# A recurrence over blocks of tokens: block transfers by column halves, and the border of a block run like its inside

## The reference, cut to what matters

```
Wx = einsum('bti,hi->bth', x, W)              # x: normalised tokens
Wx = batchnorm(Wx) * gamma + beta
def step(yt, wx_t):
    yt = sigmoid(wx_t + yt @ V.T)
    return (yt, yt)
_, ys = lax.scan(step, zeros, swapaxes(Wx, 0, 1))
out = x1 + ys                                 # x1: the residual stream, 16 images of 128 x 16384
```

## Time and profile before

| | |
|---|---|
| time, median of 3 runs (lowest, highest) | 5048.64 us (5047.34, 5053.07) |
| the profiled execution: time | 5051.68 us |
| its span | 5049.9 us |
| PE busy, granted clock over the span | 96%, 0.989 |
| DVE, ACT, POOL busy | 80%, 77%, 75% |
| the recurrence's 1024 steps | about 3879 to 5006 us of the span, then the last store |

### The profile page before, as it was taken

How to read it: one execution, slowest core, us unless ns; L and a number is a source line. 1 busy time by engine, 2 the same in 40 slices (tenths; PEclk the granted TensorE clock), 3 DMA queues, 4 the chain that set the end, 5 groups by cost and what they waited for, 6 DMA issues and landing times. The chain is left out here.

```text
span 5049.9 us, 147380 instructions
## 1 busy us (share of the span) xinstructions
PE 4850.0 (96%) x38766; PEld 4491.2 (89%) x38766; DVE 4028.0 (80%) x13465; ACT 3900.6 (77%) x10328; POOL 3787.5 (75%) x5133
## 2 busy tenths in 40 slices
PE   7999999999999999999999999999986999999996
PEld 6799999999999999999999999899876999999996
DVE  7899999999999999999999999999964444444442
ACT  5788888888888888888888888888874666666664
POOL 6688887888887878888887888888762666666764
PEclk9999999999999999999999999999998999999998
DMA  2355555555555545555554555555475689888897
GB/s 59 94 147 149 143 146 143 145 145 146 144 147 143 148 142 146 146 142 149 143 148 141 147 144 147 143 146 149 134 199 223 167 243 262 211 240 243 248 244 158
DMA packets 1692439, 821.25 MB, mean 163 GB/s; under 512 B 1095328, under 2 KB 1623584, under 8 KB 1689936
## 3 DMA queue, kind: packets, MB, share of 16 engines
q1 hardware_dynamic: 1690528, 816.80, 57.5%
q10 hardware_dynamic: 1584, 0.79, 0.1%
HBM read 413.17 MB, written 270.01 MB: 135 GB/s over the span
## 5 line engine op out<-in xcount | busy, mean ns | idle before, releaser
L502 POOL TENSOR_TENSOR x_t<-x_t,y 128x512 f32<-128x512 f32 x512 | 769.3, 1527 | 425.4 <-ACT y L436 425.4
L436 ACT ACTIVATE y<-bank,zbias 128x128 f32<-128x128 f32 x2112 | 776.9, 368 | 387.7 <-PE bank L402 255.5
L458 DVE TENSOR_TENSOR th_t<-x_t,bank 128x512 f32<-128x512 f32 x528 | 528.6, 1042 | 645.0 <-PE bank L373 563.8
L402 PE MATMUL bank<-y,VT 128*128 128x128 f32 x4216 | 869.2, 289 | 11.0 <-issue 10.3
L380 PE MATMUL bank<-th_t,WzT 128*128 128x128 f32 x4224 | 805.2, 277 | 13.0 <-DVE th_t L458 12.8
L662 PEld LDWEIGHTS bank<-WqT,xh 128*128 128x128 f32 x4096 | 538.7, 192 | 245.3 <-issue 245.3
L402 PEld LDWEIGHTS bank<-y,VT 128*128 128x128 f32 x4216 | 671.6, 189 | 59.7 <-issue 13.2
L787 ACT ACTIVATE thT<-bank,srstd 128x128 f32<-128x128 f32 x1920 | 548.6, 369 | 191.2 <-POOL srstd L878 190.9
L805 ACT ACTIVATE onT<-bank,orstd 128x128 f32<-128x128 f32 x1920 | 548.9, 369 | 135.9 <-POOL orstd L897 135.3
L380 PEld LDWEIGHTS bank<-th_t,WzT 128*128 128x128 f32 x4224 | 635.5, 193 | 20.3 <-DVE th_t L458 20.2
L919 POOL TENSOR_TENSOR rstd<-veps,minus_half 128x4 f32<-128x4 f32 x512 | 531.4, 1038 | 76.2 <-POOL veps L915 1.2
(11 more groups left out here) (150 smaller groups left out, 11285.5 us busy)
## 6 DMA issues: line engine op xcount, KB each, us to landing
xin<-in_x SPq DMA_DIRECT2D x512, 256.0 KB, 2.9
qin<-q_image SPq DMA_DIRECT2D x512, 256.0 KB, 2.7
x2in<-in_x SPq DMA_DIRECT2D x512, 256.0 KB, 2.9
x_scratch<-x1o SPq DMA_DIRECT2D x1024, 128.0 KB, 2.1
out<-x_t SPq DMA_DIRECT2D x256, 512.0 KB, 6.6
r_t<-r_scratch SPq DMA_DIRECT2D x51, 32.0 KB, 2.1
r_scratch<-rS SPq DMA_DIRECT2D x3, 256.0 KB, 20.9
r_scratch<-rS ACTq DMA_DIRECT2D x3, 256.0 KB, 21.5
```

Of the source, the lines that this page charges most:

```text
L402: pe.matmul(z_b[c][g % 2][:, u * CC:(u + 1) * CC], VT[:], last, start=False, stop=(u == GS - 1), skip_group_check=True).then_inc(pre_ps[c], 1)
L436: act.activation(y[c][:, g % RING, u, :], z_b[c][g % 2][:, u * CC:(u + 1) * CC], ACT.Sigmoid, bias=zbias[:]).then_inc(y_sb[c], 1)
L458: dve.tensor_tensor(th_t[c][:, g % 2].rearrange("p u (x q) -> p u x q", x=XP), x1_t[q][:, c * CC:(c + 1) * CC, h * GS:(h + 1) * GS].rearra ...
L502: pool.tensor_tensor(dst, dst, y[c][:, g % RING, :, :].rearrange("p u (x q) -> p q x u", x=XP), ALU.add).then_inc(slot_free[c], 1)
```

## The change

The load of a block is split into two DMAs, one for each column half, with semaphores of their own, and the stores count on a semaphore for each half. SP starts the stores of half 0 (sequences 0 to 7) when half 0's last add is done, and those of half 1 after half 1's; each half's load waits for its own half's stores. DVE waits for `x1_in` of each half at that half's first `scale`.

The border of a block is issued like its inside: `z_piece` of the next block's first group stands between the V matmuls of the last group, and the r pieces of the second group after its second step. DVE's order of work is the same as before, written without the special cases. The broadcast of r (`r_piece`) is one matmul for a group and half, as it was.

```
-            sp.dma_start(x1_t[p][:], x1_s[bass.ds(blk, 1)].rearrange("o c s t -> (o c) s t")).then_inc(x1_in[p], 16)
+            cols = slice(c * CC, (c + 1) * CC)
+            sp.dma_start(x1_t[p][:, cols, :], x1_s[bass.ds(blk, 1), :, cols].rearrange("o c s t -> (o c) s t")).then_inc(x1_in[p][c], 16)
...
-                    if stored is not None:
-                        sp.wait_ge(out_st[p], stored)
-                        settle(sp)
-                    load_x1(sp, blk, p)
+                    for c in range(2):
+                        if stored is not None:
+                            sp.wait_ge(out_st[p][c], stored)
+                            settle(sp)
+                        load_x1(sp, blk, p, c)
...
                     for c in range(2):
                         sp.wait_ge(slot_free[c], w * SWEEP + blk * NG + NG + RING)
                         settle(sp)
-                    src = x1_t[p][:].rearrange("c (b j) t -> c b j t", j=J)
-                    for b in range(B):
-                        sp.dma_start(out_v[bass.ds(blk, 1), :, b].rearrange("o c j t -> (o c) j t"), src[:, b]).then_inc(out_st[p], 16)
+                        for b in range(c * B // 2, (c + 1) * B // 2):
+                            sp.dma_start(out_v[bass.ds(blk, 1), :, b].rearrange("o c j t -> (o c) j t"), src[:, b]).then_inc(out_st[p][c], 16)
...
-                            if g + 1 < n:
+                            if g + 1 < n or ahead:
                                 z_piece(g + 1, u, c)
-                            if u == 1 and (g + 2 < n or ahead and g + 2 == n):
+                            if u == 1 and (g + 2 < n or ahead):
                                 r_piece(g + 2, c)
-                if ahead:
-                    for u in range(GS):
-                        for c in range(2):
-                            z_piece(n, u, c)
-                    for c in range(2):
-                        r_piece(n + 1, c)
...
-                    if g in (0, n) and c == 0:
-                        dve.wait_ge(x1_in[q], 16 * (loaded if q == p else loaded + 1 - p))
+                    if g in (0, n):
+                        dve.wait_ge(x1_in[q][c], 16 * (loaded if q == p else loaded + 1 - p))
```

More of the change, by code:

```diff
@@ L127, in build @@
         r_in = [sem(f"r_in{p}") for p in range(2)]
-        x1_in = [sem(f"x1_in{p}") for p in range(2)]
-        out_st = [sem(f"out_st{p}") for p in range(2)]
+        x1_in = [[sem(f"x1_in{p}{c}") for c in range(2)] for p in range(2)]
+        out_st = [[sem(f"out_st{p}{c}") for c in range(2)] for p in range(2)]
         start_ok = [sem(f"start_ok{c}") for c in range(2)]
@@ L308, in build, with load_x1 @@
         y0 = [yb[:].rearrange("p (x b j) -> p x b j", x=XP, j=J // XP) for yb in y_start]
-        def load_x1(sp, blk, p):
-            sp.dma_start(x1_t[p][:], x1_s[bass.ds(blk, 1)].rearrange("o c s t -> (o c) s t")).then_inc(x1_in[p], 16)
+        def load_x1(sp, blk, p, c):
+            cols = slice(c * CC, (c + 1) * CC)
+            sp.dma_start(x1_t[p][:, cols, :], x1_s[bass.ds(blk, 1), :, cols].rearrange("o c s t -> (o c) s t")).then_inc(x1_in[p][c], 16)
         def scan_dma(sp):
@@ L334, in loads @@
                     load_r(blk, p)
-                    if stored is not None:
-                        sp.wait_ge(out_st[p], stored)
-                        settle(sp)
-                    load_x1(sp, blk, p)
+                    for c in range(2):
[3 more added lines that the diff above has]
+                        load_x1(sp, blk, p, c)
                 def store(blk, p):
+                    src = x1_t[p][:].rearrange("c (b j) t -> c b j t", j=J)
                     for c in range(2):
@@ L353, in scan_dma @@
                         store(2 * k + p, p)
-                        loads(2 * k + 2 + p, p, w * SWEEP + WARM + (2 * k + p + 1) * NG, (stores + k + 1) * 16 * B)
+                        loads(2 * k + 2 + p, p, w * SWEEP + WARM + (2 * k + p + 1) * NG, (stores + k + 1) * 8 * B)
                 for p in range(2):
@@ L357, in scan_dma @@
                 for p in range(2):
-                    sp.wait_ge(out_st[p], (stores + NB // 2) * 16 * B)
-                    settle(sp)
+                    for c in range(2):
+                        sp.wait_ge(out_st[p][c], (stores + NB // 2) * 8 * B)
+                        settle(sp)
         def scan_tensor(pe):
@@ L466, in block_steps @@
                 for g in range(n):
-                    if g + 2 < n or ahead and g == n - 1:
+                    if g + 2 < n or ahead:
                         for c in range(2):
[L469 to L472, removed]
+                            scale(g + 2, c)
             for c in range(2):
@@ L580, in _ @@
             sp.wait_ge(gram_ps, B * NC)
-            load_x1(sp, NB - 1, 1)
+            for c in range(2):
+                load_x1(sp, NB - 1, 1, c)
             store_r(sp, 0)
```

## The result

The changed kernel takes 5064.9 us (median of 8 runs), the kernel before 5048.4 us in 8 runs beside it: the ratio is 1.0031, with a 95% interval from 1.0020 to 1.0042. It is slower by 0.31%, some 16 us. One disturbed run of 9189.5 us is left out of the comparison.

What follows compares the result with a forecast made beforehand. PE's order and the transfers were taken to bind at once. Blocks 1 to 14 +12.0, block 0 +0.4, block 15 -2.8, last stores -1.5: together +8.1 us on the median 5048.6, so 5057 us; range 5036 to 5068.

Steps and rivals of the forecast that it cites:

- border like inside, block there: Block border issued like its inside, nothing else late: 67.1 us a block, giving PE back 3.5 us a block.
- first store's issue: SP's first store at A + 1.73, A being the start of POOL's first add in a block's last group.
- gain of the transfers by halves: First load need not wait for the last store's landing: 0.7 us sooner, bounds 0 and about 1.4 us.
- half 1's scale starts: DVE starts half 1's scale at A + 66.0 (A: start of POOL's first add in a block's last group).
- 8 landing blocks, clock up: Eight blocks with no branch back ahead stop 3.4 us for half 1 in the last group: 70.5 us each.
- stop at a branch: PE's stop at its loop's end, at six borders, grows from 1.7 to 2.7 us; growth between 0 and 1.8.
- 6 branch blocks, clock up: Six blocks behind a branch back reach half 1 after it is ready, no second stop: 67.1 + 2.7 us each.
- slow stretches: PE's clock falls to 1.2 GHz at nearly every new stop, 1.3 us each; bounds 0 and 1.5.
- The clock that stays up: Rival: PE's clock does not fall at the new stops, all blocks take 70.5 us: 5043 us; chance 0.15.
- the transfers overlap better: Rival: half 1's landing moves 2.4 us, not 0.7, and the stop shrinks to 1.7 us: 5029 us; chance 0.13.
- The half loads at half speed: Rival: half-row loads run slowly, the load's 23 us become 43, each block grows by 20: +280 us; chance 0.02.
- The case of no gain in the transfers: Rival: transfers gain nothing, branch stop of 3.9 us, a full-price clock fall each time: 5072 us; chance 0.10.

Runs made afterwards that it cites:

- half of the stores: The changed kernel with 8 of each block's 16 stores left out, so half the output is never written and loads go out earlier: 5006.5 us, ratio 0.9914.
- the order alone: The kernel before, with whole-block transfers, given only the changed PE program (new order of the border): 5106.9 us, ratio 1.0113.
- the halves alone: The changed kernel, with transfers by halves, given PE's program of before (old order of the border): 5045.7 us, ratio 0.9990.
- half 1 late: The changed kernel with half 1's z matmuls and r piece in a block's last group put behind the last V matmul: 5029.0 us, ratio 0.9961.

## Why the prediction was right, and where its sizes were off

The mechanism is as it was put: what the border gave back, the block's landing and the branch took, and the slow clock behind the new stops added to it. The point, 5057 us, was 8 us short: +8 was forecast, +16 came. The result lies just above the band from 5048 to 5064 us to which the forecast gave 0.60, and almost midway between the point and the 5072 us of a rival; the prediction held a change within 0.2% (0.46) a little likelier than a slower kernel (0.40). So the sign and the path are right, and the size isn't. For the profiled execution the steps compare like this:

| step | forecast | measured |
|---|---|---|
| border like inside, block there (half of the stores) | 67.1 us a block | 67.2 |
| first store's issue | A + 1.73 | A + 1.76 |
| gain of the transfers by halves | 0.7 us | 0.6 |
| half 1's scale starts | A + 66.0 | A + 66.15 |
| from that start to the next A, clock up | 1.05 + 3.4 = 4.45 | 4.53 (three blocks) |
| 8 landing blocks, clock up | 70.5 | 70.65 (66.12 + 4.53) |
| stop at a branch | 2.7 | 3.2 |
| 6 branch blocks, clock up | 67.1 + 2.7 = 69.8 | 70.7 |
| slow stretches | 14, 1.3 us each: 18.2 | 9, 16.2 us together |
| blocks 1 to 14 | +12.0 | +16.4 |
| up to block 0's A | +0.4 | +2.3 |
| block 15 | -2.8 | -3.6 |
| last store | -1.5 | -1.5 |

**The term that failed in size is the branch back.** The stop was to grow from 1.7 to 2.7 us, taken between 0 and 1.8 more; it grew to 3.2, near the upper end. That is 0.5 us in each of six blocks, +3.1. And that PE comes to half 1 there after it is ready, and does not stop again, was not quite so: where no slow stretch follows the branch (blocks 9 and 11), the last group takes 4.65 us (4584.20 to 4588.85) and not 4.2, because PE is still early. It waits 0.27 us for half 1 there, and the group is some 0.5 us longer in all, +1.0 for the two. In the other four the last group takes 4.2 us. Some 0.2 us more a block are left, mostly in the group behind the stop, which takes 4.45 us beside it (block 9: 7.48 - 3.03). Together +5.2.

The runs that show it: the order alone has the same 19.4 us at branches, the halves alone 9.7. The trace shows why, in its records of the transfers that load instructions (q8). At each branch one of them brings 16 KB. Behind block 4 it begins at 4231.74, 0.65 us after PE stopped; in the kernel before it began at 4229.69, 0.60 us ahead of the stop at 4230.29. It is the lone entry early in each of these rows of 40 slices (the first pair of lines is the stretch from 4231.0 to 4234.6 after the change, the second that from 4229.5 to 4232.4 before it; q8's line gives transfers, MB and share):

```profile
GB/s 0 0 0 0 0 0 0 0 182 0 0 0 0 0 0 0 0 0 0 0 0 0 0 0 0 0 0 0 0 0 0 37 179 256 213 213 219 225 213 216
...
q8 instruction: 1, 0.02, 1.8%
...
GB/s 0 0 226 0 0 0 0 0 0 0 0 0 0 0 0 0 0 0 0 0 0 0 0 0 0 0 0 0 0 0 0 0 0 0 0 71 208 240 226 212
...
q8 instruction: 1, 0.02, 1.9%
```

PE starts again 2.6 to 3.1 us after the start of that load, at all 48 branches of the eight kernels here that have the loop. That the load is of PE's own program is inferred from its place; with the loop and half of the stores gone such loads still come every 10 to 20 us, and PE stops for none. What the change moved is the load against the stop: before, it began 0.5 to 1.2 us ahead of PE's stop, now 0.4 to 0.65 us after it. On average that is 1.4 us of cover gone, of the 1.8 us by which the work ahead of the branch was to shrink; the forecast had taken 1.0. The Trainium skill (Runtime: NRT & Kernel Launch, "Instruction fetch mechanics") prefers loops written out, since a taken branch whose target isn't held has to fetch it. The trace agrees, with one 16 KB load at each stop, but the written-out loop alone gained nothing here (5072.1 us): the landing took its place.

**The landing blocks** cost 0.15 us more each than forecast without the slow clock, +1.2: half 1's scale starts at A + 66.12 on average in the eight, and from there it is 4.53 us to the next A.

**The clock** went the other way. Nine of fourteen stops had a slow stretch behind them, not all: the longest, block 8's of 3.80 us, had none, nor those of 3.34 and 3.44 us (blocks 4 and 14) and the branches behind blocks 8 and 10 with 3.0 us, while block 6's 2.65 us had one. But on average each costs more than the 1.3 us taken, and a little more than the bound of 1.5. In the five landing blocks that have one it is 1.55 us, counted from half 1's scale to the next A. Behind the branches the first group takes 4.45 us beside the stop without a slow stretch, 6.04 us with one of 3.4 us, and 7.0 to 7.1 with one of 6.8: 1.6 and 2.6 us more. Together 5 x 1.55 + 2 x 1.6 + 2 x 2.6 = 16.2 us, 2.0 less than forecast. +5.2 + 1.2 - 2.0 = +4.4, which is the difference of 16.4 and 12.0.

**The rest** is the way into block 0, where a slow stretch of 6.8 us stands in the profiled execution after the change (3867.6 to 3874.4) and none in that before, and the first part, which took 6.4 us less in that execution (the r loads ahead of the recurrence go out at 3859.08 and not at 3865.50) though the change does not touch it. From there on the changed kernel takes 16.4 + 2.3 - 3.6 - 1.5 = 13.6 us longer, so the profiled execution lies 7 us over that of before. That this is near the forecast's +8 is luck. The last 3 us up to the 16 of the medians are not shown, since only one execution was recorded: the mean granted clock of the other runs is 0.984 to 0.986 against 0.987, and more slow stretches would fit.

**The rivals.** The clock that stays up is out: nine slow stretches stand in blocks 1 to 14, and they cost 16.2 us. That the transfers overlap better is out: 0.6 us and not 2.4. The half loads at half speed are out: store start to scale is 64.4 us, not 20 us more (its sum made 43 us of a doubled 23). The case of no gain in the transfers has the right sign, but not its terms: the transfers gained 0.6 us, the branch's stop was 3.2 and not 3.9 us, and five stops of fourteen had no slow stretch.

## What to carry to other kernels

When an order of work is made denser, look up when each operand is first wanted, not only how many instructions are saved: here the dense border asked for half 1 six microseconds earlier, and the time that it saves was kept only where half 1's use was put behind the last V matmul. Of several stops that follow one another, taking one away can move the wait to the next: the loop written out gave nothing by itself (5072.1 us), and 20 to 30 us once the landing was out of the way (from 5029.0 to 5009.5 us with half 1 late, from 5006.5 to 4976.5 with half of the stores). Work that seems to stand idly ahead of a loop's branch may be what hides it.

## What the runs showed of the hardware that was not expected

A branch back of PE with almost no work ahead of it stops 2.9 to 3.6 us (five kernels here), with ten matmuls ahead of it 1.4 to 2.1 us, and with half of these (half 1 late) 2.2 to 2.5 us. In all of them PE starts again 2.6 to 3.1 us after a 16 KB load of instructions begins. After a stop the slow clock sometimes lasts 6.8 us and not 3.4: twice in blocks 1 to 14 of the changed kernel, four times with the loop written out (13 slow stretches), and eleven times with the order alone (14), among them behind all eight of its stops of 5.1 to 6.8 us. In the changed kernel a stretch of 3.4 us costs 1.4 to 1.6 us, one of 6.8 us 2.6. Whether one comes after a stop of some 3 us differs between blocks that look alike in the trace. Three small loads of 32 KB each between a block's last store and its load delay the landing by 1.3 us. And two half loads, whose rows are pieces of a longer row, land as fast as the whole: 64.4 us from the first store to the scale against 65.0.
